# First attention of a decoder block: the inverse softmax denominators kept as two fp16 parts, a step's operands fetched one step earlier, the dense weights' rounding later in a step

## What is computed

```
x = x + attention_1(layernorm(x))        # 32 query heads of 32, 8 key/value heads, sign weights, softmax
x = x + layer_2(layernorm(x))            # a second, causal attention with 16 heads, and a gated MLP
x = x + dense(layernorm(x))              # 1024 x 1024 weights and low-rank adapters
```

## Time and profile before

| | |
|---|---|
| time, median of 3 runs | 945.73 us (944.59 to 948.35) |
| the profiled execution's own time | 947.53 us |
| its span in the trace | 945.8 us |
| granted TensorE clock, mean | 0.934 |
| PE / DVE / ACT / POOL busy | 834.6 / 648.4 / 418.0 / 305.9 us |

### The profile page before, as it was taken

The page is one execution under the profiler, slowest core; times in us unless marked ns, Lnnn a source line. Parts: engine busy times, 40 slices in busy tenths (PEclk is TensorE's granted clock), DMA queues, the critical chain, the costliest instruction groups (busy, mean ns, idle before and its releaser), DMA issues.

```text
span 945.8 us, 15035 instructions
## 1 busy us (share of the span) xinstructions
PE 834.6 (88%) x5594; PEld 450.7 (48%) x5594; DVE 648.4 (69%) x1348; ACT 418.0 (44%) x819; POOL 305.9 (32%) x297
## 2 busy tenths in 40 slices
PE   4899689999999999899996778877799999999977
PEld 2675233333343333356664323236556656656633
DVE  7865367787887874467786667435678778679661
ACT  4466415676676767223343356533232332332310
POOL 2000004676676767310100135342232232232210
PEclk9899799999999999999997578768799999999997
DMA  8664522141322222111225431110001001001011
GB/s 329 235 231 137 167 73 90 60 111 47 108 79 77 88 67 96 57 45 42 79 68 167 182 97 59 47 43 17 1 1 47 16 30 45 10 35 34 7 38 45
DMA packets 75625, 75.78 MB, mean 80 GB/s; under 512 B 37493, under 2 KB 63877, under 8 KB 74918
## 3 DMA queue, kind: packets, MB, share of 16 engines
q1 hardware_dynamic: 74998, 68.77, 23.8%
q10 hardware_dynamic: 560, 6.12, 1.7%
HBM read 53.56 MB, written 21.04 MB: 79 GB/s over the span
## 4 chain that ended last, share of the span: by engine, by line
PE 67%; DVE 11%; ACT 7%; DMA 5%; SPq 4%; issue 4%; POOL 2%; POOLq 0%; DVEq 0%; ACTq 0%; PEldq 0%
PE psum L1625 6%; PE psum L1707 6%; PE psum L2013 6%; PE psum L1988 5%; PE psum L1758 5%; PE psum L1747 5%; PE psum L1949 4%; PE psum L1815 4%; PE psum L1822 3%; PE psum L1768 3%; PE psum L1915 3%; DMA ops<-q_scr 2%; SPq L536 2%; PE psum L1893 2%; PE psum L2001 2%
## 5 line engine op out<-in xcount | busy, mean ns | idle before, releaser
L1271 DVE TENSOR_REDUCE m_neg<-psum 128x1 f32<-128x512 f32 x256 | 164.5, 682 | 43.6 <-PE psum L1707 41.6
L911 ACT ACTIVATE region_x<-psum 128x512 f32<-128x512 f32 x256 | 140.8, 596 | 64.0 <-PE psum L1747 63.8
L679 POOL TENSOR_TENSOR region_p<-region_x 128x2048 f32<-128x2048 f32 x32 | 145.3, 4539 | 42.0 <-ACT region_x L911 25.7
L1707 PE MATMUL psum<-ops 96*128 96x512 f16 x256 | 97.0, 387 | 13.1 <-DMA ops<-q_scr 11.8
L1747 PE MATMUL psum<-ops 98*128 98x512 f16 x256 | 95.7, 381 | 1.7 <-ACT region_x L911 1.5
L1625 PE MATMUL psum<-region_x,region_w 128*128 128x512 f16 x320 | 77.0, 398 | 3.0 <-ACT region_w L849 3.0
L1707 PEld LDWEIGHTS psum<-ops 96*128 96x128 f16 x256 | 24.8, 97 | 93.5 <-DVE m_neg L1271 64.0
L2013 PE MATMUL psum<-ynT,region_w 128*128 128x128 f32 x512 | 63.5, 288 | 6.3 <-ACT ynT L1055 6.3
L1758 PE MATMUL psum<-region_x,v_g 128*32 128x512 f32 x512 | 67.8, 604 | 0.0
L2013 PEld LDWEIGHTS psum<-ynT,region_w 128*128 128x128 f32 x512 | 61.9, 203 | 10.0 <-ACT ynT L1055 10.0
L1815 PE MATMUL psum<-sign_o_all,region_a 128*128 128x512 f16 x256 | 60.2, 387 | 4.3 <-DVE region_p L1338 2.8
(11 more groups left out here) (236 smaller groups left out, 1485.4 us busy)
## 6 DMA issues: line engine op xcount, KB each, us to landing
ops<-q_scr SPq DMA_DIRECT2D x48, 128.0 KB, 2.6
region_a<-in_x SPq DMA_DIRECT2D x8, 512.0 KB, 8.5
region_a<-in_w_q SPq DMA_DIRECT2D x8, 512.0 KB, 7.1
region_w<-in_w_o SPq DMA_DIRECT2D x8, 512.0 KB, 4.0
region_w<-in_kern SPq DMA_DIRECT2D x16, 256.0 KB, 2.9
kern_scr<-region_w SPq DMA_DIRECT2D x32, 128.0 KB, 1.9
region_p<-in_x SPq DMA_DIRECT2D x8, 512.0 KB, 3.6
region_a<-kern_scr ACTq DMA_DIRECT2D x1, 4096.0 KB
```

Source lines behind the costliest of these rows:

```text
L679: pool.tensor_tensor(pair_sum[:, n], prob_a[:, 2 * n], prob_a[:, 2 * n + 1], ALU.add).then_inc(pair_ready, 1)
L911: act.activation(prob_a[:, kt, j, :], psum[:, (0, 4, 5)[(16 * i + n) % 3], :], ACT.Exp, scale=A_SCALE).then_inc(p_ready, 1)
L1271: dve.tensor_reduce(m_neg[:, i % 3, n:n + 1], psum[:, 1 + (16 * i + n) % 3, :], AX_X, ALU.max, negate=True).then_inc(s_max, 1)
L1707: pe.matmul(psum[:, 1 + (16 * i + n) % 3, :], qa_op[u][0:A_MAX, j, qt * P:(qt + 1) * P], k_op[u][0:A_MAX, :], start=True, stop=True).then_ ...
```

## The change

- The inverse denominators are written as two fp16 parts, side by side in one 128 x 128 operand: a rounding (`round_inverse`) and a masked difference (`inverse_parts`). The four matmuls of `spread_inverse` are fp16 instead of fp32. VectorE gets two instructions of 128 x 128 in each step, at n = 12 and n = 13. ScalarE converts the matrix `spread` once, after step 0, and VectorE makes a mask of 128 x 1 once, ahead of step 0. POOL builds `spread` with additions in place of copies, once.
- `load_qk(k + 3)` is issued in round k of SP's queue, right behind `load_max(k + 1)`; before, it was issued behind `store_kern(k)`, `load_kern(k + 1)` and, every third step, a load of the MLP weights (`ctx`).
- `kern_hi` moves from n = 2 to n = 6, `kern_lo` from n = 5 to n = 9.

```diff
+DEN_GAIN = 1.0 / S
-        den_inv, den_sel, spread = ynT[:, 0, :], ynT[:, 1, :].rearrange("p (k e) -> p k e", k=QT), ynT[:, 2:, :]
+        den_inv, den_sel, spread_32 = ynT[:, 0, :], ynT[:, 1, :].rearrange("p (k e) -> p k e", k=QT), ynT[:, 2:, :]
+        den_hi, den_parts, spread = hi_st[:, 0:P], hi_st[:, P:2 * P], lo_st[:].rearrange("p (k n) -> p k n", k=QT)
+        den_mask = mvs[:, 0:1]
...
-            load_max(1)
-            store_kern(0)
-            load_kern(1)
-            load_qk(3)
-            load_max(2)
-            store_kern(1)
-            load_kern(2)
-            for k in range(2, NI - 2):
-                load_qk(k + 2)
+            for k in range(NI - 2):
                 load_max(k + 1)
+                if k + 3 < NI:
+                    load_qk(k + 3)
                 store_kern(k)
                 load_kern(k + 1)
-                if k % 3 == 0:
+                if k >= 3 and k % 3 == 0:
...
# scalar
                     exp(k, n)
-                    if n == 2:
+                    if n == 6:
                         kern_hi(k)
...
             step(0, done=0)
+            act.wait_ge(made, 14)
+            act.wait_ge(staged_out[0], K_STORED + 64)
+            act.activation(lo_st[:], spread_32.rearrange("p k n -> p (k n)"), ACT.Copy, scale=DEN_GAIN).then_inc(spread_ready, 1)
             step(1, done=1)
...
# vector
+            dve.tensor_reduce(den_mask, ident[:, 1:P:A_HD // QT], AX_X, ALU.add, negate=True)
...
+            def round_inverse(i):
+                dve.wait_ge(den_rec, 3 * i + 1)
+                dve.tensor_copy(den_hi, den_inv).then_inc(den_rec, 1)
+
+            def inverse_parts(i):
+                dve.wait_ge(den_rec, 3 * i + 2)
+                dve.scalar_tensor_tensor(den_parts, den_hi, den_mask, den_inv, ALU.mult, ALU.add).then_inc(den_rec, 1)
...
                     if n == 11 and done > 0:
                         invert(k - 1)
-                    if n == 5:
+                    if n == 12 and done > 0:
+                        round_inverse(k - 1)
+                    if n == 13 and done > 0:
+                        inverse_parts(k - 1)
+                    if n == 9:
                         kern_lo(k)
...
# tensor
-                pe.wait_ge(den_rec, i + 1)
+                pe.wait_ge(den_rec, 3 * i + 3)
                 for q in range(QT):
-                    mm = pe.matmul(psum[:, 7, q * P:(q + 1) * P], spread[:, q, :], den_inv, start=True, stop=True)
+                    mm = pe.matmul(psum[:, 7, q * P:(q + 1) * P], spread[:, q, :], den_parts, start=True, stop=True)
```

More of the change, by code:

```diff
@@ L336, in build_program @@
         vg_ready = sem("vg_ready")
-        pair_ready, den_done, den_spread = sem("pair_ready"), sem("den_done"), sem("den_spread")
+        pair_ready, den_done, den_spread, spread_ready = sem("pair_ready"), sem("den_done"), sem("den_spread"), sem("spread_ready")
         o_copied, den_rec, att_ready, att_hi_ready, att_lo_ready = sem("o_copied"), sem("den_rec"), sem("att_ready"), sem("att_hi_ready"), sem("att_lo_ready")
@@ L698, in _ @@
             for n in range(QT):
-                pool.memset(den_sel[:, n, n * A_HD // QT:(n + 1) * A_HD // QT], 1.0).then_inc(made, 1)
-                pool.tensor_copy(spread[:, n, :].rearrange("p (j e) -> p j e", j=A_REP),
-                                 ident[:, n * A_HD // QT:P:A_HD].unsqueeze(2).broadcast_to([P, A_REP, A_HD])).then_inc(made, 1)
+                pool.memset(den_sel[:, n, n * A_HD // QT:(n + 1) * A_HD // QT], DEN_GAIN).then_inc(made, 1)
+                pool.tensor_tensor(spread_32[:, n, :].rearrange("p (j e) -> p j e", j=A_REP),
+                                   *(ident[:, n * A_HD // QT + m:P:A_HD].unsqueeze(2).broadcast_to([P, A_REP, A_HD]) for m in range(2)),
+                                   ALU.add).then_inc(made, 1)
             pool.sem_inc(att_lo_ready, 1)
@@ L1329, in _ @@
             invert(NI - 1)
+            round_inverse(NI - 1)
+            inverse_parts(NI - 1)
             normalise(NI - 1)
@@ L1801, in _ @@
             step(1, done=1)
-            pe.wait_ge(made, 14)
+            pe.wait_ge(spread_ready, 1)
             for k in range(2, NI - 2):
```

## The result

The changed kernel takes 992.64 us (median of 4 runs, 987.76 to 994.55), the kernel before 945.16 beside it: ratio 1.0462, 95% interval 1.042 to 1.0503. (The two medians alone would give 1.0502, the upper end of that interval; the same kernel run again, e8, gave 1.0464.) The forecast was 982 in a range of 970 to 1003.

The account below looks back on a forecast made before the run. PE was taken to bound the first attention, with DVE close behind; 36.4 + 3.6 - 0.7 - 3.0 - 0.8 = +35.5 us gave 983.0 on the profiled run, 981.2 on the median; forecast 982, range 970 to 1003.

Parts of the forecast that it names:

- blocked at full clock: Likeliest case, chance 0.50: POOL's pair holds kern_lo while PE's clock stays at 1.00; 978 to 990 us.
- blocked with the clock falling: Rival, chance 0.31: kern_lo held and PE's pauses lower its clock, up to 1.7 us a step; 992 to 1004 us.
- signs of being wrong: kern_lo at 0.68 us beside a pair, or granted clocks of 0.5 inside steps, putting the time near 1000.
- PE bounds, and DVE from slot 11 to slot 1 is without slack: First attention: PE busy 14.67 of 14.67 us; DVE work added from slot 11 to next slot 1 delays PE.
- `kern_lo` is blocked by the pair and ends 0.55 behind it: In steps 1 to 13, at slot 9, kern_lo waits out POOL's pair and lasts 3.5 to 3.8 us.
- +2.8 a step, 36.4 in all: Steps 1 to 13: PE's slot 1 comes 3.5 us late, less 0.67 for the faster spread.
- The two small instructions at 0.2 each: DVE's rounding and parts at slots 12 and 13 take back 0.4 us of the spread's 0.67 gain.
- The spread: Four fp16 matmuls on PE take 0.22 us instead of 0.89, a gain of 0.67 us each time.
- Loads and the ACT wait, -3.0 and -0.8: Earlier loads end five PE waits for queries, 3.0 us; step 15's wait for a weights tile goes, 0.8 us.
- Step 0, +3.6: In step 0 POOL's pair holds kern_lo, so DVE's queue frees at 162.84 instead of about 159.2.
- The end, -0.7: Steps 14 and 15: no cost counted for kern_lo; the faster spread in step 15 saves 0.7 us.
- The clock, 0 in the likeliest case: PE's clock was taken to stay full despite a pause of over 2 us a step, adding nothing.

Follow-up runs that it names:

- e1: The changed kernel with kern_hi at slot 4 and kern_lo at slot 6, the rest kept: 939.86 us, ratio 0.9902 to the kernel before.
- e3: The changed kernel with POOL's first pair of each step made to wait for kern_lo: 1050.01 us, ratio 1.1078 to the kernel before.
- e9: The changed kernel with POOL adding each pair as two half-size instructions: 955.43 us, ratio 1.0073 to the kernel before.
- e2: The kernel before with only the rounding moved, kern_hi to slot 6 and kern_lo to slot 9: 1009.01 us, ratio 1.0616.
- e7: The kernel before with only the loads issued one step ahead: ratio 1.003.
- e4: The changed kernel with PE repeating a score matmul ten times at slot 12 to fill its pause: 986.69 us, ratio 1.0403 to the kernel before.
- e10: The kernel with POOL's pair waiting for kern_lo, plus the inverse's upper part made by a second reciprocal from PSUM: 954.22 us, ratio 1.0058 to the kernel before.

## Why the prediction was right, point by point

The block of `kern_lo` was right in place and size. But of the cases it is not the likeliest one, "blocked at full clock" (0.50, 978 to 990 us), that came; it is the first rival, "blocked with the clock falling" (0.31, 992 to 1004), at 992.64. The forecast of 982 is 10.6 us short, and the time lies inside the range because that was drawn up over this rival. One of the signs of being wrong, granted clocks of 0.5 inside the steps, did come, in about half of them.

- **PE bounds, and DVE from slot 11 to slot 1 is without slack:** right. PE's waits for maxima are 39.7 us in all, 1.3 before.
- **`kern_lo` is blocked by the pair and ends 0.55 behind it:** right, 3.68 us in 13 of the steps. Shown by e1 (0.68 with no pair), e3 (0.68 at slot 9 with the pair moved) and e9 (1.52 with the pair halved). The condition as the prediction has it, two SBUF inputs, was too narrow: the cast, with one, is held too. In the changed kernel that shows only in steps 14 and 15, where it takes 3.1 us of DVE's time.
- **+2.8 a step, 36.4 in all:** measured 17.45 - 14.67 = +2.78 at full clock, the last window 17.37 - 14.1 = +3.27; 12 x 2.78 + 3.27 = 36.6.
- **The two small instructions at 0.2 each:** 0.13 and 0.26 of the queue. The spread: 0.22, right.
- **Loads and the ACT wait, -3.0 and -0.8:** the four longer steps of before (15.24 to 15.81, +3.5 over 14.67 together) are gone. But e2 has no such wait with the old loads: the steps that are 3 us longer would have removed it by themselves. As a gain of the edit the term was wrong at this place, and by itself the edit is a small loss (e7). The sentence that the later `kern_hi` covers the later weights tile was right, and e7 shows what it costs without that cover.
- **Step 0, +3.6:** measured +6.1. e4, with the clock mostly kept, has +5.1. `kern_lo` took 4.3 us there and ended 0.56 us behind the pair (163.36 against 162.80), as computed, but the pair began 0.46 us later than before (158.30 against 157.84). Some 2 us more are the clock's and the pause's there, and I have not split them further.
- **The end, -0.7:** -1.4: from the last transpose of the maxima to the projection 21.32 us, 22.72 before. With the later start of 0.2 the parts give 36.6 - 3.5 + 7.5 + 6.1 - 1.4 + 0.2 = 45.5 of the +45.6.
- **The clock, 0 in the likeliest case:** this is the term that was mis-sized. The 13 steps after the first take 234.3 us; at 17.45 they would take 226.8. So +7.5, and with the part of step 0's excess about +10. The named rival said "In half of the steps +11": 7 of these 13 steps have a dip, of 0.8 to 2.0 us each, where it had up to 1.7. My argument against it, "the pause here is shorter", did not hold: a pause of 2.40 us was enough, in about half of the cases. With PE kept busy (e4) the attention is +35.8 against the forecast +35.5. That close an agreement is in part luck: counted from the first transpose it is +37.0, with +5.1 in the first window in place of 3.6 and less at the end.

What stays open: why the same pause of 2.40 us is followed by a dip in some steps and not in others. At 239.46 PE comes out of a pause of 2.39 us and the step stays at 1.00. Both profiles of the changed kernel have, from the fourth step on, two steps with a dip and two without, in turn. In e2, with the same pause of 2.39 or 2.40 us, 12 of the 13 windows behind the first have a dip. In e9 and e10, where PE's longest waits for maxima in these windows are 0.3 and 0.7 us, none has. No run varied the pause's length alone.

## What to carry to other kernels

Before moving a DVE instruction with two tensor inputs in SBUF, lay POOL's timeline beside its new place: here three slots made 0.68 us into 3.68 and the kernel 4.6% slower, and the same change with `kern_lo` at slot 6 is 1% faster. That holds for casts too, and for moving POOL's work onto them (e3). A way out that needs no new order is an instruction that isn't held, as the reciprocal from PSUM in e10, or to cut POOL's long instruction into pieces (e9). And a change in the order of a queue is costed with what falls back in it: loads that come earlier made another one late.

## What the runs showed of the hardware

- A DVE instruction that is held by POOL ended a fixed time behind it, short for short ones: 0.55 us behind for the 128 x 512 one (0.68 when free), 0.15 for the masked difference at 128 x 128 (0.33 free), 0.08 for the cast (0.20 free). That is 0.12 to 0.18 less than each takes when free. Its row in the timeline begins where it would have begun, so the hold reads as busy time.
- A cast with a single SBUF input was held like the others: 2.05 us in e3, and 1.38 and 2.13 us at the end of the changed kernel.
- Not held were the maxima, the 128 x 128 reciprocal with its input in PSUM, whether its result was fp32 (0.94) or fp16 (0.93), and the 128 x 48 reciprocal from SBUF (0.45). Nor was `normalise`, with one input in PSUM and one in SBUF, under the pair from 192.42 to 196.97:

```profile
195.93 0.68 DVE L1296 TENSOR_TENSOR region_w<-region_w,psum 128x512 f32<-128x512 f32 x1
```

- An instruction that begins first isn't held: `kern_lo` of steps 14 and 15 began 0.53 us before a pair and took 0.75 and 0.81 us.
- It goes the other way too: POOL's copy of the values waits for DVE's held `kern_lo` to finish (0.76 us in place of 0.29), and in e9 the second half of a pair does (5.12 in place of 4.68 for both).
- How soon behind a pause PE's clock is low differs. After 2.40 us the first two matmuls lasted 0.39 and 0.42 and only the third 0.61 (at 221.21 in after), or the first lasted 0.61 already (at 201.75 in after, and at 217.96 in e2, where the granted clock was 1.00 up to the pause). After pauses of 3.7 to 4.2 us in e3 the first always lasted 0.61.

The timeline of PE in e3:

```profile
205.16 0.61 PE L1726 MATMUL psum<-ops 96*128 96x512 f16 x1 [4.15 <-DVE m_neg L1274]
```
